# Three parts of a split product share one block of turned weights

## The chip, the cores and the metric

One core of a Trainium2 chip runs the whole program. The metric is the device time of one execution in microseconds (us). The parts named here are TensorE (matmuls), VectorE, ScalarE, GpSimd, and SyncE, whose queue issues all DMAs of this kernel, the DMA transposes among them.

## The reference

A decoder block over 16 batches of 100 tokens with 128 features. It has three parts, each followed by a residual sum and a layer norm: a self-attention of one head, a cross-attention, and a feed-forward part with product keys (8 heads, the 8 best of 1024 experts). The change is in the cross-attention:

```
q = layernorm(x) @ Wq                       # 16 heads of 64, per batch 100 tokens
k, v = split(layernorm(ctx) @ Wkv)          # ctx: 1444 rows of 128 features a batch
q = q * (1 + scale) + shift
attn = softmax(q @ k^T / 8)                 # 16 heads x 100 queries x 1444 keys
out = (attn @ v) @ Wout
```

The inputs are float32. The kernel works with the normed context itself in place of k and v (Wk is folded into the queries, Wv and Wout into one matrix), and holds each float32 number x as two float16 numbers, high = f16(x) and low = f16(x - high). A product of two such numbers is taken as three: high x high, high x low and low x high.

## The kernel before

`front` does the self-attention and prepares the first batch's context, `cross` does the cross-attention, `ffn` the rest. `cross` goes through 208 query tiles, 13 a batch: a batch has 16 x 100 = 1600 queries, so 12 tiles have 128 and the last has 64. Tile t is number i = t % 13 of its batch b. The order of work on each engine is written out by hand as one loop over t, with semaphores between the engines:

- TensorE, `scores(t)`: nine matmuls of up to 512 columns into three of six banks of PSUM, the 1444 scores of 128 queries.
- VectorE, `maximum(t)` (L887): the row maximum, and a small bias from it (L889).
- ScalarE, `exponent(t)` (L823): e32 = exp(score + bias), float32, two buffers. `high_half(t)` (L831): its float16 copy into p[., 0, .], three buffers.
- GpSimd for i in 0, 3, 4, 7 (L785), VectorE for the nine others (L896), a step later: `low_half(t)`, e32 minus the high half, into p[., 1, .].
- SyncE, `turn_high(t)` and `turn_low(t)` (L736, L742): two DMA transposes, which put 12 blocks of 128 keys by 128 queries each into pT, a ring of six tiles. 1444 keys are 11 blocks and a rest of 36; the rest of block 12 is zero.
- TensorE, `values(t)` (L999, L1000, L1003), four steps later: 12 blocks x 3 matmuls, which sum the context weighted with the turned weights into a quarter of one bank. L1003 of the first block waits for the low turn.
- ScalarE, `take_values` (L840): after each group of four tiles it copies that bank to uT; the next group's first matmul waits for this. The groups start at tiles 0, 4, 8 and 12 of a batch.

Between these go query jobs for the next batch (TensorE, then four copies on ScalarE, L850, L859, then GpSimd, L777), output jobs for the batch before (TensorE L965, VectorE L906, L910), and the next contexts: `context_load` (L519, L521, behind the turns of tile 0), statistics on VectorE (L534, L542, L547), `context_rstd` and `context_norm` on GpSimd, `context_hi` on ScalarE behind tile 4, `context_lo` on GpSimd at tile 5, and `turn_context` (L728) behind the turns of tiles 5 and 6. SyncE has one queue in this fixed order: an issue that waits holds all behind it.

The context's rows lie so that partition p has rows 11p to 11p + 10 in blocks 0 to 10. The last 36 rows lie in block 11 on partitions 0 to 35. `rows_of(n)` gives the partitions of block n in use: 128, or 36.

Of the kernel before, what the change touches and what calls it, by code (L numbers as in the profile page):

```python
# [6 lines left out]
F16 = mybir.dt.float16  # L7
# [16 lines left out]
HQ = H * S  # L24
PW = NTILE * P
NM = (HQ + P - 1) // P
LN3 = 1.0986122886681098
# [460 lines left out]
class Context:  # L488
# [3 lines left out]
    def __init__(self, sb, sem):  # L492
        self.raw = [sb(f"raw{i}", [P, NTILE, D]) for i in range(2)]
        self.cst = sb("cst", [P, NTILE, 6])
        self.cmv = [sb(f"cmv{i}", [P, NTILE, 2]) for i in range(2)]
        self.cve = sb("cve", [P, NTILE])
        self.crs = [sb(f"crs{i}", [P, NTILE]) for i in range(2)]
        self.xh = sb("xh", [P, NTILE, D])
        self.xa_hi = [sb(f"xa_hi{i}", [P, NTILE, D], F16) for i in range(2)]
        self.xa_lo = [sb(f"xa_lo{i}", [P, NTILE, D], F16) for i in range(2)]  # L500
        self.ctx_ld = [sem(f"ctx_ld{i}") for i in range(2)]
        self.init_done, self.ctx_stat, self.ctx_rstd, self.xh_done = (sem(n) for n in ("init_done", "ctx_stat", "ctx_rstd", "xh_done"))
        self.xa_hi_done, self.xa_lo_done = sem("xa_hi_done"), sem("xa_lo_done")
        self.pv_done = sem("pv_done")

        self.dve_waited = sem("dve_waited")


def context_init(pool, c):

    pool.memset(c.xh[:, :, :], 1.0).then_inc(c.init_done, 1)
    for i in range(2):
        pool.memset(c.cmv[i][:, :, :], 1.0).then_inc(c.init_done, 1)


def context_load(sp, c, a, bt):

    src = a["ctx_1024"][bass.ds(bt.index(), 1), :, :].rearrange("a t d -> (a t) d")
    sp.dma_start(c.raw[bt.par][:, 0:TF, :],  # L519
                 src[0:TF * P, :].rearrange("(p j) d -> p j d", j=TF)).then_inc(c.ctx_ld[bt.par], 16)  # L520
    sp.dma_start(c.raw[bt.par][0:TR, TF, :], src[TF * P:T, :]).then_inc(c.ctx_ld[bt.par], 16)  # L521


def context_stats(dve, c, bt, part):

    if part == 0:
        dve.wait_ge(c.ctx_ld[bt.par], bt.val(16, 32 - 16 * bt.par))
        if bt.off >= 2:
            dve.wait_ge(c.xh_done, bt.val(1, -1))
            dve.wait_ge(c.ctx_rstd, bt.val(1, 0))  # L530
# [26 lines left out]
def context_norm(dve, c, bt, part):  # L557
    if part == 0:
        dve.wait_ge(c.ctx_rstd, bt.val(1, 1))
        if bt.off >= 1:  # L560
            dve.wait_ge(c.xa_lo_done, bt.val(1, 0))
    for n in range(4 * part, 4 * part + 4):
        r = rows_of(n)
# [11 lines left out]


def context_lo(pool, c, bt):
    pool.wait_ge(c.xa_hi_done, bt.val(1, 1))
# [6 lines left out]
def rows_of(n):  # L585
    return P if n < TF else TR

# [75 lines left out]
def cross(nc, a, m, ps):  # L663
# [6 lines left out]
    with ExitStack() as ctx:  # L670
# [3 lines left out]
        def sem(name):  # L674
# [12 lines left out]
        e32 = [sb(f"e32_{i}", [P, T]) for i in range(E_BUF)]  # L687
        p = [sb(f"p{i}", [P, 2, PW], F16) for i in range(P_BUF)]
        pT = sb("pT", [P, RING, 2 * NTILE, P], F16)
        uT = sb("uT", [D, HQ])  # L690
# [3 lines left out]

        cx = m["context"]
        xa_hi, xa_lo, xh_done, xa_hi_done, xa_lo_done, pv_done, dve_waited = (
            cx.xa_hi, cx.xa_lo, cx.xh_done, cx.xa_hi_done, cx.xa_lo_done, cx.pv_done, cx.dve_waited)
# [3 lines left out]
        s_rdy, max_done, bias_done = sem("s_rdy"), sem("max_done"), sem("bias_done")  # L701
        e_done, hi_done, lo_dve, lo_pool = sem("e_done"), sem("hi_done"), sem("lo_dve"), sem("lo_pool")
        xT_ld = sem("xT_ld")
# [18 lines left out]
        def _(sp):  # L722
# [8 lines left out]
            def turn_high(t):  # L731
                rows = tile_rows(t % NM)
                sp.wait_ge(hi_done, t + 1)
                if t >= RING:
                    sp.wait_ge(pv_done, t - RING + 1)
                sp.dma_start_transpose(pT[:, t % RING, 0:NTILE, 0:rows.stop - rows.start],  # L736
                                       p[t % P_BUF][rows, 0, :]).then_inc(pT_hi_ld[t % RING], 16)

            def turn_low(t):
                rows = tile_rows(t % NM)  # L740
                sp.wait_ge(lo_pool if t % NM in POOL_LO else lo_dve, lo_of(t))
                sp.dma_start_transpose(pT[:, t % RING, NTILE:2 * NTILE, 0:rows.stop - rows.start],  # L742
                                       p[t % P_BUF][rows, 1, :]).then_inc(pT_lo_ld[t % RING], 16)

# [18 lines left out]
        def _(pool):  # L763
# [16 lines left out]
            def low_half(t):  # L780
                rows = tile_rows(t % NM)
                pool.wait_ge(hi_done, t + 1)
                if t >= P_BUF:
                    pool.wait_ge(pT_lo_ld[(t - P_BUF) % RING], 16 * ((t - P_BUF) // RING + 1))
                pool.tensor_tensor(out=p[t % P_BUF][rows, 1, 0:T], in0=e32[t % E_BUF][rows, :], in1=p[t % P_BUF][rows, 0, 0:T],  # L785
                                   op=ALU.subtract).then_inc(lo_pool, 1)

# [5 lines left out]
            for k in range(P_BUF):  # L793
                pool.memset(p[k][:, :, T:PW], 0.0).then_inc(pad_done, 1)
            queries_lo(0, 0)
# [21 lines left out]
        def _(act):  # L817
            def exponent(t):
                rows = tile_rows(t % NM)
                act.wait_ge(bias_done, t + 1)  # L820
                if t >= E_BUF:
                    act.wait_ge(lo_pool if (t - E_BUF) % NM in POOL_LO else lo_dve, lo_of(t - E_BUF))
                act.activation(e32[t % E_BUF][rows, :], score_banks(t)[rows, 0:T], ACT.Exp,  # L823
                               bias=bias[rows, t % N_BUF:t % N_BUF + 1]).then_inc(e_done, 1)

            def high_half(t):
# [3 lines left out]
                act.wait_ge(e_done, t + 1)  # L830
                act.activation(p[t % P_BUF][rows, 0, 0:T], e32[t % E_BUF][rows, :], ACT.Copy).then_inc(hi_done, 1)  # L831

# [48 lines left out]
        def _(dve):  # L881
# [9 lines left out]
            def low_half(t):  # L891
                rows = tile_rows(t % NM)
                dve.wait_ge(hi_done, t + 1)
                if t >= P_BUF:
                    dve.wait_ge(pT_lo_ld[(t - P_BUF) % RING], 16 * ((t - P_BUF) // RING + 1))
                dve.tensor_tensor(out=p[t % P_BUF][rows, 1, 0:T], in0=e32[t % E_BUF][rows, :], in1=p[t % P_BUF][rows, 0, 0:T],  # L896
                                  op=ALU.subtract).then_inc(lo_dve, 1)

# [26 lines left out]
            def layer_norm(b):  # L925
                dve.wait_ge(y_rstd, b + 1)
                dve.tensor_scalar(x2[:, b, :], acc[:, :], ymv[:, 0:1], yrs[:, 0:1], ALU.subtract, ALU.mult).then_inc(y_norm, 1)

            for part in range(4):
                context_stats(dve, cx, Batch(None, 1), part)  # L930
            for part in range(3):
                context_norm(dve, cx, Batch(None, 1), part)
            for t in range(ALL_TILES + DRAIN):
# [8 lines left out]
                if i in STAT_SLOTS and b + 2 < B:  # L942
                    context_stats(dve, cx, Batch(None, b + 2), STAT_SLOTS.index(i))
                if i == 6 and b or t == ALL_TILES + DRAIN - 1:
                    layer_norm(b - 1)

        @block.tensor
        def _(pe):
# [39 lines left out]
            def values(t):  # L988
# [6 lines left out]
                w = tile_cols(i).stop - tile_cols(i).start  # L995
                for n in range(NTILE):
                    hi, lo = xa_hi[b % 2][:, n, :], xa_lo[b % 2][:, n, :]
                    ph, pl = pT[:, t % RING, n, 0:w], pT[:, t % RING, NTILE + n, 0:w]
                    pe.matmul(out, hi, ph, start=n == 0, stop=False)  # L999
                    pe.matmul(out, lo, ph, start=False, stop=False)  # L1000
                    if n == 0:
                        pe.wait_ge(pT_lo_ld[t % RING], 16 * (t // RING + 1))
                    last = pe.matmul(out, hi, pl, start=False, stop=n == NTILE - 1)  # L1003
                last.then_inc(pv_done, 1)
# [618 lines left out]
```

## Time and profile before

| | us |
|---|---|
| median of 3 runs | 1376.27 (1375.0 to 1378.77) |
| the profiled execution | 1373.3 |
| its span | 1371.5 |
| TensorE matmuls busy | 1176.9 (86%) |
| VectorE busy | 1116.3 (81%) |
| ScalarE busy | 849.1 (62%) |
| GpSimd busy | 618.9 (45%) |
| SyncE's turns of the weights | 416 issues |

The profile is of one execution. Busy time is the union of an engine's instructions. A matmul's duration there is that of its way through the engine (about 0.22 us), and several are under way at once, so the distance between two starts tells what one costs. SyncE only issues, so it has no busy time; its issues are in the timeline with their durations. The idle time before an instruction stands behind it in brackets with what ended it.

### The profile page before, as it was taken

What the parts mean: (1) busy time and instruction counts of PE and PEld (TensorE: products, weight loads), DVE (VectorE), ACT (ScalarE), POOL (GpSimd) and SP (SyncE); (2) the same over time, 40 slices, a digit from 0 to 9 for tenths busy, and PEclk for the clock granted to TensorE, in tenths of its full rate; (3) what the DMA queues carried; (4) which work ended last, traced back from release to release, by engine and by line L of the source; (5) the groups of instructions that cost most, each with busy time, mean ns of one, the idle gap of its engine ahead of it and who ended that gap; (6) DMA issues with size and microseconds to landing.
All of it is one profiled execution on the core that took longest, in us unless ns stands there. A gap on an engine that the chain in (4) does not pass through costs nothing. (4 is left out here: it accounts for less than half of the span.)

```text
span 1371.5 us, 32769 instructions
## 1 busy us (share of the span) xinstructions
PE 1176.9 (86%) x13174; PEld 923.8 (67%) x13174; DVE 1116.3 (81%) x2700; ACT 849.1 (62%) x994; POOL 618.9 (45%) x445
## 2 busy tenths in 40 slices
PE   3567999998999999999999999999997547777788
PEld 2454677776777767777776777677775526776678
DVE  5886888887889888897888888888885278999984
ACT  0347778877778786777778778887773531222121
POOL 2254856566475666656476575667230000000000
PEclk9768999999999999999999999999998665666656
DMA  7016999999999999999999999999997200000000
GB/s 150 1 38 131 193 199 198 190 196 194 195 188 197 195 191 197 196 189 192 201 195 194 194 193 196 191 190 190 188 190 139 69 1 1 5 5 5 5 5 6
DMA packets 695185, 191.77 MB, mean 140 GB/s; under 512 B 681045, under 2 KB 692601, under 8 KB 694905
## 3 DMA queue, kind: packets, MB, share of 16 engines
q1 hardware_dynamic: 695032, 189.67, 81.5%
q8 instruction: 104, 1.70, 0.5%
q14 instruction: 49, 0.39, 0.1%
HBM read 18.92 MB, written 0.82 MB: 14 GB/s over the span
## 5 line engine op out<-in xcount | busy, mean ns | idle before, releaser
L1003 PE MATMUL ps<-pT,xa_hi 128*128 128x128 f16 (+1 forms) x2496 | 415.9, 217 | 27.2 <-DMA pT<-p 26.9
L999 PE MATMUL ps<-pT,xa_hi 128*128 128x128 f16 (+1 forms) x2496 | 417.5, 217 | 21.4 <-ACT uT L840 20.1
L823 ACT ACTIVATE e<-ps,bias 128x1444 f32<-128x1444 f32 (+1 forms) x208 | 305.4, 1468 | 194.4 <-DVE bias L889 194.1
L887 DVE TENSOR_REDUCE nmax<-ps 128x1 f32<-128x1444 f32 (+1 forms) x208 | 344.5, 1656 | 95.3 <-PE ps L985 94.2
L1000 PE MATMUL ps<-pT,xa_lo 128*128 128x128 f16 (+1 forms) x2496 | 417.6, 217 | 0.0
L831 ACT ACTIVATE p<-e 128x1444 f16<-128x1444 f32 (+1 forms) x208 | 294.5, 1416 | 8.5 <-DMA pT<-p 0.5
L896 DVE TENSOR_TENSOR p<-e,p 128x1444 f16<-128x1444 f32 x144 | 268.1, 1862 | 11.4 <-ACT p L831 7.8
L999 PEld LDWEIGHTS ps<-pT,xa_hi 128*128 128x128 f16 x2496 | 242.8, 98 | 49.4 <-issue 33.6
L785 POOL TENSOR_TENSOR p<-e,p 128x1444 f16<-128x1444 f32 x64 | 187.5, 2930 | 180.3 <-ACT p L831 178.4
L1003 PEld LDWEIGHTS ps<-pT,xa_hi 128*128 128x128 f16 x2496 | 242.7, 98 | 34.1 <-DMA pT<-p 33.8
L1000 PEld LDWEIGHTS ps<-pT,xa_lo 128*128 128x128 f16 x2496 | 242.7, 98 | 13.1
L983 PE MATMUL ps<-xT_hi,q_hi 128*128 128x512 f16 (+1 forms) x624 | 229.7, 368 | 8.0 <-DMA xT_lo<-xa_lo 7.2
L984 PE MATMUL ps<-xT_hi,q_lo 128*128 128x512 f16 (+1 forms) x624 | 229.6, 368 | 0.0
L985 PE MATMUL ps<-xT_lo,q_hi 128*128 128x512 f16 (+1 forms) x624 | 229.3, 368 | 0.0
L777 POOL TENSOR_TENSOR q_lo<-q,q_hi 128x400 f16<-128x400 f32 x64 | 102.7, 1605 | 181.5 <-ACT q_hi L859 181.5
L564 POOL TENSOR_SCALAR xh<-raw,cmv,crs 128x127 f32<-128x127 f32 x168 | 169.0, 1019 | 0.0
L1516 PE MATMUL ps<-mv_hi,oneh 128*128 128x16 f16 (+1 forms) x832 | 109.7, 215 | 44.9 <-DVE mv_lo L1437 44.9
L1516 PEld LDWEIGHTS ps<-mv_hi,oneh 128*128 128x128 f16 (+1 forms) x832 | 109.1, 175 | 47.8 <-DVE mv_lo L1437 47.3
L1153 POOL TENSOR_TENSOR comb<-top 128x512 f32<-128x512 f32 (+1 forms) x13 | 13.7, 1070 | 220.9 <-DVE top L1339 220.9
L1517 PEld LDWEIGHTS ps<-mv_lo,oneh 128*128 128x128 f16 (+1 forms) x832 | 109.0, 175 | 1.1 <-issue 1.0
L1517 PE MATMUL ps<-mv_lo,oneh 128*128 128x16 f16 (+1 forms) x832 | 109.4, 214 | 0.0
L985 PEld LDWEIGHTS ps<-xT_lo,q_hi 128*128 128x128 f16 x624 | 61.3, 98 | 66.4 <-issue 1.3
(219 smaller groups left out, 1794.9 us busy)
## 6 DMA issues: line engine op xcount, KB each, us to landing
raw<-in_ctx SPq DMA_DIRECT2D x16, 704.0 KB
pT<-p SPq DMA_TRANSPOSE x416, 4.5
f_wq<-in_L_ffn_w_q SPq DMA_DIRECT2D x1, 1024.0 KB, 4.9
f_wqt<-in_ffn_wq_t SPq DMA_DIRECT2D x2, 512.0 KB, 7.0
x_tok<-in_x SPq DMA_DIRECT2D x1, 800.0 KB
out_x<-ost SPq DMA_DIRECT2D x6, 128.0 KB, 1.8
wk_t<-in_wk_t SPq DMA_DIRECT2D x1, 512.0 KB, 5.9
wq_t<-in_wq_t SPq DMA_DIRECT2D x1, 512.0 KB, 8.2
```

The lines of the kernel that those rows point to most:

```text
L823: act.activation(e32[t % E_BUF][rows, :], score_banks(t)[rows, 0:T], ACT.Exp, bias=bias[rows, t % N_BUF:t % N_BUF + 1]).then_inc(e_done, 1)
L831: act.activation(p[t % P_BUF][rows, 0, 0:T], e32[t % E_BUF][rows, :], ACT.Copy).then_inc(hi_done, 1)
L887: dve.tensor_reduce(nmax[rows, k:k + 1], score_banks(t)[rows, 0:T], AX_X, ALU.max, negate=True).then_inc(max_done, 1)
L896: dve.tensor_tensor(out=p[t % P_BUF][rows, 1, 0:T], in0=e32[t % E_BUF][rows, :], in1=p[t % P_BUF][rows, 0, 0:T], op=ALU.subtract).then_inc ...
L983: pe.matmul(out, hi, xT_hi[b % 2][:, keys], start=True, stop=False)
L984: pe.matmul(out, lo, xT_hi[b % 2][:, keys], start=False, stop=False)
L985: last = pe.matmul(out, hi, xT_lo[b % 2][:, keys], start=False, stop=True)
L999: pe.matmul(out, hi, ph, start=n == 0, stop=False)
L1000: pe.matmul(out, lo, ph, start=False, stop=False)
L1003: last = pe.matmul(out, hi, pl, start=False, stop=n == NTILE - 1)
L1516: pe.matmul(dst, oneh[0:j, :, s], mv_hi[0:j, 0:nb, s], start=True, stop=False)
L1517: last = pe.matmul(dst, oneh[0:j, :, s], mv_lo[0:j, 0:nb, s], start=False, stop=True)
```

## The change

The products of the last 36 keys are high x high, high x low and low x high as well, and need three matmuls of a block that is three quarters zero. After the change one block holds all three: the weights' rest as high, high, low in three stretches of 36 columns, and the context's rest as high, low, high on the partitions 0 to 35, 36 to 71 and 72 to 107. One matmul sums them. p becomes one row of 23 blocks: 11 high, the shared block, 11 low. `turn_high` turns 11 blocks, `turn_low` the other 12.

For this the context's last 36 rows are loaded three times, onto three stretches of partitions, and the statistics and the norm run on 108 partitions. VectorE makes `xa_mix` once a batch: the normed rest, less its high half where the column `lo_rows` is -1 (partitions 36 to 71). ScalarE copies the weights' 36 columns in a second instruction, twice side by side. The low half is done in two instructions.

```diff
+COPIES = 3
+PB = 2 * TF + 1
...
 def context_load(sp, c, a, bt):
...
-    sp.dma_start(c.raw[bt.par][0:TR, TF, :], src[TF * P:T, :]).then_inc(c.ctx_ld[bt.par], 16)
+    for k in range(COPIES):
+        sp.dma_start(c.raw[bt.par][k * TR:(k + 1) * TR, TF, :], src[TF * P:T, :]).then_inc(c.ctx_ld[bt.par], 16)
...
+def context_mix(dve, c, bt):
+    dve.wait_ge(c.xa_hi_done, bt.val(1, 1))
+    if bt.off >= 2:
+        dve.wait_ge(c.pv_done, NM * (bt.off - 1))
+    dve.scalar_tensor_tensor(out=c.xa_mix[bt.par][:, :], in0=c.xa_hi[bt.par][:, TF, :], scalar=c.lo_rows[:, 0:1],
+                             in1=c.xh[:, TF, :], op0=ALU.mult, op1=ALU.add).then_inc(c.xa_mix_done, 1)
...
 def rows_of(n):
-    return P if n < TF else TR
+    return P if n < TF else COPIES * TR
...
-        p = [sb(f"p{i}", [P, 2, PW], F16) for i in range(P_BUF)]
-        pT = sb("pT", [P, RING, 2 * NTILE, P], F16)
+        p = [sb(f"p{i}", [P, PB * P], F16) for i in range(P_BUF)]
+        pT = sb("pT", [P, RING, PB, P], F16)
...
             def turn_high(t):
...
-                sp.dma_start_transpose(pT[:, t % RING, 0:NTILE, 0:rows.stop - rows.start],
-                                       p[t % P_BUF][rows, 0, :]).then_inc(pT_hi_ld[t % RING], 16)
+                sp.dma_start_transpose(pT[:, t % RING, 0:TF, 0:rows.stop - rows.start],
+                                       p[t % P_BUF][rows, 0:TF * P]).then_inc(pT_hi_ld[t % RING], 16)
             def turn_low(t):
...
-                sp.dma_start_transpose(pT[:, t % RING, NTILE:2 * NTILE, 0:rows.stop - rows.start],
-                                       p[t % P_BUF][rows, 1, :]).then_inc(pT_lo_ld[t % RING], 16)
+                sp.wait_ge(again_hi, t + 1)
+                sp.dma_start_transpose(pT[:, t % RING, TF:PB, 0:rows.stop - rows.start],
+                                       p[t % P_BUF][rows, TF * P:PB * P]).then_inc(pT_lo_ld[t % RING], 16)
...
             def high_half(t):
...
-                act.activation(p[t % P_BUF][rows, 0, 0:T], e32[t % E_BUF][rows, :], ACT.Copy).then_inc(hi_done, 1)
+                act.activation(p[t % P_BUF][rows, 0:TF * P], e32[t % E_BUF][rows, 0:TF * P], ACT.Copy).then_inc(hi_done, 1)
+                if t >= P_BUF:
+                    act.wait_ge(pT_lo_ld[(t - P_BUF) % RING], 16 * ((t - P_BUF) // RING + 1))
+                n = rows.stop - rows.start
+                act.activation(p[t % P_BUF][rows, TF * P:TF * P + 2 * TR].rearrange("q (c k) -> q c k", c=2),
+                               e32[t % E_BUF][rows, TF * P:T].rearrange("q (c k) -> q c k", c=1).to_broadcast([n, 2, TR]),
+                               ACT.Copy).then_inc(again_hi, 1)
...
             def low_half(t):
...
-                dve.tensor_tensor(out=p[t % P_BUF][rows, 1, 0:T], in0=e32[t % E_BUF][rows, :], in1=p[t % P_BUF][rows, 0, 0:T],
-                                  op=ALU.subtract).then_inc(lo_dve, 1)
+                for out, keys in (((TF + 1) * P, slice(0, TF * P)), (TF * P + 2 * TR, slice(TF * P, T))):
+                    if out < (TF + 1) * P:
+                        dve.wait_ge(again_hi, t + 1)
+                    ins = dve.tensor_tensor(out=p[t % P_BUF][rows, out:out + keys.stop - keys.start], in0=e32[t % E_BUF][rows, keys],
+                                         in1=p[t % P_BUF][rows, keys], op=ALU.subtract)
+                ins.then_inc(lo_dve, 1)
...
+                if i == 6 and b + 1 < B:
+                    context_mix(dve, cx, Batch(None, b + 1))
...
             def values(t):
...
-                for n in range(NTILE):
+                if i == 0:
+                    pe.wait_ge(cx.xa_mix_done, b + 1)
+                for n in range(TF):
...
-                    last = pe.matmul(out, hi, pl, start=False, stop=n == NTILE - 1)
+                    pe.matmul(out, hi, pl, start=False, stop=False)
+                last = pe.matmul(out, xa_mix[b % 2][:, :], pT[:, t % RING, TF, 0:w], start=False, stop=True)
```

GpSimd's `low_half` is split in the same way. The column `lo_rows` is made once in `context_init` by three small GpSimd instructions.

## Rows read from the trace of the kernel before

**Rows 1.** The page's granted TensorE clock, in tenths, over 40 slices of the span.

```profile
PEclk9768999999999999999999999999998665666656
```

**Rows 2.** Busy time of one window: PE, PEld, DVE, ACT, POOL, clock, DMA share, GB/s.

```profile
104.80:1050.80 946.00, 893.16 (x10616) 676.47 (x10617) 794.03 (x1319) 734.81 (x810) 557.61 (x369) 1.00 1.14 191
```

**Rows 3.** Waits from 122 to 1050.8 us: engine and line, total us, times, longest.

```profile
ACT e L823 <- DVE bias L889: 183.3, 147, 3.0
POOL p L785 <- ACT p L831: 166.9, 59, 9.4
...
PE ps L1003 <- DMA pT<-p: 26.9, 31, 1.7
PE ps L999 <- ACT uT L840: 20.1, 35, 1.0
...
POOL p L785 <- DMA pT<-p: 1.8, 1, 1.8
DVE p L896 <- DMA pT<-p: 1.4, 2, 0.9
```

**Rows 4.** Waits of the SyncE queue in the same window.

```profile
SPq L736 <- ACT p L831: 66.3, 62, 2.8
```

**Rows 5.** Timeline of SyncE at a context load: start us, duration us, line.

```profile
531.73 0.87 SPq L519 DMA_DIRECT2D raw<-in_ctx  x1
532.64 0.40 SPq L521 DMA_DIRECT2D raw<-in_ctx  x1
533.14 2.54 SPq L736 DMA_TRANSPOSE pT<-p  x1
```

**Rows 6.** SyncE's lines over the span: duration ns min/median/max, first and last start.

```profile
L736 SPq DMA_TRANSPOSE pT<-p x208: 1246/1762/3280, 114.7 to 1043.1; - x104
L742 SPq DMA_TRANSPOSE pT<-p x208: 1302/1808/4261, 117.6 to 1044.7; - x104
L521 SPq DMA_DIRECT2D raw<-in_ctx x16: 384/398/407, 4.2 to 826.7; - x16
```

**Rows 7.** Timeline of SyncE at the two turns of a batch's last tile.

```profile
580.26 3.25 SPq L742 DMA_TRANSPOSE pT<-p  x1
583.60 1.25 SPq L736 DMA_TRANSPOSE pT<-p  x1
584.91 1.43 SPq L742 DMA_TRANSPOSE pT<-p  x1
```

**Rows 8.** Timeline of TensorE at three waits, idle time in brackets.

```profile
555.01 0.22 PE L999 MATMUL ps<-pT,xa_hi 128*128 128x128 f16 x1 [0.78 <-ACT uT L840]
...
555.18 0.22 PE L999 MATMUL ps<-pT,xa_hi 128*128 128x128 f16 x1
...
533.64 0.19 PE L999 MATMUL ps<-pT,xa_hi 128*128 128x64 f16 x1 [0.48 <-ACT uT L840]
...
533.73 0.19 PE L999 MATMUL ps<-pT,xa_hi 128*128 128x64 f16 x1
...
569.99 0.23 PE L1003 MATMUL ps<-pT,xa_hi 128*128 128x128 f16 x1 [1.43 <-DMA pT<-p]
```

**Rows 9.** Timeline of ScalarE ahead of the wait at 533.64.

```profile
531.53 1.48 ACT L823 ACTIVATE e<-ps,bias 128x1444 f32<-128x1444 f32 x1
...
536.45 0.22 ACT L840 ACTIVATE uT<-ps 128x64 f32<-128x64 f32 x1
536.64 1.41 ACT L831 ACTIVATE p<-e 128x1444 f16<-128x1444 f32 x1
```

**Rows 10.** Timeline of VectorE ahead of the wait at 555.01.

```profile
544.24 0.17 DVE L906 RECIPROCAL ry<-ps 100x1 f32<-100x1 f32 x1 [0.22 <-PE ps L965]
...
545.55 0.85 DVE L534 BATCH_NORM_STATS2 cst<-raw 128x6 f32<-128x128 f32 x4
546.33 1.64 DVE L887 TENSOR_REDUCE nmax<-ps 128x1 f32<-128x1444 f32 x1
...
548.08 2.79 DVE L896 TENSOR_TENSOR p<-e,p 128x1444 f16<-128x1444 f32 x1
```

## What the change does to the time: the prediction

> **What bounds the kernel now.** First the granted clock over the span [rows 1], then the window of the stage at full clock [rows 2]. The reader is to see that the middle 946 us of 1371.5, the cross-attention stage, are one steady state: TensorE at the full 2.4 GHz, busy for 893.2 us (94%), and the DMA share above 1 all the while. VectorE is busy for 794.0 us (84%), ScalarE for 734.8 us (78%). The change touches this stage and, by two small loads, the one before it.
>
> Next the waits of the stage [rows 3]. TensorE idles in two places only: 26.9 us before L1003, the first matmul that needs the low half of a tile's turned weights (they have not landed), and 20.1 us before L999, when the bank of values has not been emptied by ScalarE (uT). ScalarE (183.3 us of waiting for VectorE's bias) and GpSimd (166.9 us before its low halves) have room on average.
>
> The last engine to look at is SyncE's queue, which turns the weights. The view of waits gives it idle time [rows 4], but the timeline does not show it: each issue begins 0.04 to 0.1 us after the one before has ended [rows 5]. The sum agrees with the timeline. A batch has 13 turns of 1.762 us and 13 of 1.808 us [rows 6], two of the context of about the same length (3.6 us), loads of 0.87 and 0.40 us [rows 5], and some 30 gaps of 0.09 us: 46.4 + 3.6 + 1.3 + 2.7 = 54.0 us. A batch takes 946/16 = 59.1 us. The 5 us between are issues that last 3 us in place of 1.8, as the one at 580.26 [rows 7]. So I read two chains of nearly equal length: SyncE's turns, without slack, and TensorE's matmuls, which wait 3 us a batch (26.9 + 20.1 over 16). The waits for L1003 are the places where the first chain holds the second.
>
> **The change, part by part.** The sum is made against the profiled execution: 1373.3 us, span 1371.5. The median of the runs shown is 1376.3, 3.0 more; I add that at the end.
>
> *Two matmuls fewer a tile.* The 128-column value matmuls start 0.056 us apart (555.01 to 555.18 is three of them), the 64-column ones of a batch's last tile 0.03 us (533.64 to 533.73) [rows 8]. 192 tiles x 2 x 0.056 + 16 x 2 x 0.03 = 22.5 us of TensorE's time, 1.4 us a batch. All of it lies on TensorE's own chain. What takes some of it back are the waits that do not get shorter with it.
>
> *The uT waits grow.* They fall on the 5th and the 13th tile of a batch, where a group of four value tiles begins: 0.78 us at 555.01 and 0.48 us at 533.64 [rows 8]. At the 13th the bank is free when ScalarE's exponent at 531.53, which starts with no idle time before it, and the uT copy behind it are done [rows 9]. Ahead of that exponent now stands the second small copy of the high halves. ScalarE's nearest row is the 64-column uT copy at 536.45, 0.19 us before the next instruction; the long copy loses 36 of 1444 columns, 0.03 us. So ScalarE arrives 0.16 us later, TensorE 2 x 0.11 us earlier: the wait grows by 0.4 us. At the 5th tile the chain runs over VectorE, from TensorE's job at 544.24 over the statistics, the maximum, the low half at 548.08 (2.79 us) and the next maximum [rows 10] to the exponent and uT. It gets the split low half and the new mix. Four statistics of 128 columns take 0.78 us (545.55 to 546.33), 0.195 us each, 0.06 us above their columns; so the split costs 0.06 us and the mix, of 128 columns, about 0.2 us. Two value tiles of TensorE lie beside it (0.22 us), so this wait grows by 0.5 us. Together 0.9 us a batch, 14 us in all. Between these points VectorE's and ScalarE's additions (9 splits a batch, 0.16 us a tile) lie in their idle time.
>
> *The price from the Trainium skill.* Its page "VectorE: DVE Perf Modes" (section "The TRN2 errata — SBUF-src ops pay a fixed extra latency per instruction") gives ScalarE 224 cycles and VectorE about 151 cycles on top of the elements. For 72 and 36 elements that is 0.25 and 0.19 us, estimates from the page; by them the two waits would grow by 1.1 us a batch in place of 0.9, 3 us in all. No row of before shows either instruction.
>
> *SyncE's queue.* The high turn goes from 12 blocks to 11. If the issue follows the blocks, it is shorter by 1.762/12 = 0.147 us. The last tile of a batch has half the rows, and its two issues at 583.60 and 584.91 last 1.25 and 1.43 us [rows 7], 0.45 us less for half of the data, which is 0.075 us for a twelfth. And 1.25 us may be a floor, so that nothing is gained. I take 0.1 us, between the first two: 13 x 0.1 = 1.3 us a batch, 21 us in all (0 to 31). Against it stand two more loads of 18 KB a batch, 0.398 us of issue each and the gap, 0.9 us. They are issued right behind the 704 KB load, and the next turn (533.14) takes 2.54 us, 0.8 us more than the median, since it waits for that load [rows 5, 6]. The new issues fall into this time, so I price them at 0.1 us a batch; without that cover they cost 14 x 0.9 = 12.6 us. In the front stage two of them stand ahead of the attention's weights: 0 to 0.9 us, I take 0.5.
>
> *The same in the words of the skill.* "DMA: Bandwidth & Descriptors" (section "Rules for kernel authors") says to coalesce small transfers, since under 64 KB one pays mostly overhead. That speaks against three loads of 18 KB. The trace puts 0.398 us of SyncE's time on one; where it falls decides the price, and the page does not say.
>
> *The waits for the low half shrink.* SyncE's chain gets 1.2 us a batch faster. TensorE's gets 1.4 - 0.9 = 0.5 us faster. The difference, 0.7 us a batch, can come out of the 26.9 us (1.7 us a batch) of waits: 11 us at most. Since the waits come in lumps (1.43 us at 569.99), where a long issue falls, I take 9.
>
> *Edits at nothing.* ScalarE now waits for the low turn of three tiles before, as VectorE did before it wrote the same buffer. Behind it stand the next exponent and the query copies. Before the low halves the same wait cost 1.8 us on GpSimd and 1.4 us on VectorE [rows 3], and the low turn gets no later. If it bound at each group of query jobs, it would cost 0.3 us a batch. GpSimd's split hides in its 166.9 us [rows 3], and the low turn waits in SyncE's queue anyway. Statistics and norm on 108 rows in place of 36 have the same columns. Waits for the mix are satisfied tiles earlier, as it is made at tile 6 of the batch before. The FFN and what follows the stage are untouched.
>
> *Sum.* -22.5 + 14 - 9 + 0.5 = -17.0 us, 1.1 us a batch. Both chains allow it: SyncE's alone gives -19. 1373.3 - 17 = 1356; with the 3 us to the median, 1359.
>
> **Rivals.** *(A) TensorE alone sets the time.* The uT waits do not grow, as the exponent has slack, and the low-half waits shrink. For: 94% busy, and only 20.1 us of uT waits. Against: those waits end on an exponent with nothing idle before it. Then -22.5 - 9 + 0.5 = -31: 1345. Chance 0.17.
>
> *(B) Slower: SyncE's queue sets the time and the issue of a turn does not follow its blocks.* The place is the turn after the context load. The shorter high turn saves nothing (floor of 1.25 us), the two extra issues delay each turn behind them, and the queue has no idle time in which to catch up. 12.6 us in the stage and 0.9 us in front: +13.5, 1390. It decides from the point where the high turns save less than 0.9 us a batch, 0.07 us each, and the raw load no longer covers the issues. For: back-to-back issues, the 1.25 us floor. Against: a half tile's turns are shorter, and the 0.8 us beside the raw load. With half of the cover it is 1383. Chance 0.21.
>
> *(C) No change: what TensorE saves goes into waits.* The high turns save nothing and the loads are covered, so SyncE's chain stays at its length, and TensorE waits 1.4 us more a batch, at L1003 in place of L999. 1376, within 4 us. The same comes out if small instructions cost twice my price (uT waits +1.8 us a batch, -22.5 + 29 - 9 = -2). Chance 0.14.
>
> **How the numbers follow.** Forecast 0.48, A 0.17, C 0.14, B 0.21. The predicted time is the forecast's, 1359; its own range, from the SyncE term of 0.075 to 0.147 us and uT waits of 0.6 to 1.2 us a batch, is 1351 to 1367. The range for all is 1346 to 1383: it takes in most of A, all of C and the near part of B. 0.3% is 4 us, about what a measurement of this kernel tells from no change. Faster by more than that: the forecast and A, 0.65. Within: C, 0.14. Slower: B, 0.21.
>
> **What would show it.** Value matmuls 7072 in place of 7488, at the same distance. The median of L736's issue falls to about 1.66 us (0 saved: B or C; 1.61: the blocks count in full). The uT waits rise from 20 to some 34 us, the low-half waits fall from 27 to some 18. The copy of 72 columns takes about 0.2 us on ScalarE, VectorE's busy time in the stage rises by about 12 us. The turn behind the load stays near 2.5 us or falls towards 1.8, while the batch does not get longer. I am wrong if low-half waits grow (then SyncE's queue was the one bound, and its turns did not get shorter), or if uT waits stay where they are.

## The result, and the profile after

The changed kernel takes 1363.65 us (median of 4 runs, 1362.32 to 1367.09); the kernel before took 1376.36 beside it. The ratio is 0.991 (0.9885 to 0.9934): 12.7 us less. The forecast was 1359. The profiled execution of the changed kernel was the slowest of its four, 1367.1 us with a span of 1365.3, against 1373.3 and 1371.5. So the two traces differ by 6.2 us, half of what the medians do, and they are read for the places of the time, the medians for its size.

The first fence is the window of the stage after: busy time of PE, PEld, DVE, ACT, POOL, then clock, DMA share and GB/s, as in [rows 2]. The second has the waits from 122 to 1050.8 us, as in [rows 3].

```profile
104.80:1050.80 946.00, 873.56 (x10212) 660.55 (x10212) 836.80 (x1494) 757.63 (x1018) 559.62 (x433) 0.99 1.10 184
```

```profile
POOL p L811 <- ACT p L859: 172.2, 49, 9.9
ACT e L851 <- DVE bias L923: 160.6, 128, 3.5
...
PE ps L1042 <- ACT uT L874: 60.4, 48, 4.5
...
PE ps L1006 <- DVE acc L948: 2.9, 2, 1.4
...
PE ps L1046 <- DMA pT<-p: 0.9, 2, 0.7
```

L1042 is the old L999, L1046 the old L1003. TensorE is busy for 19.6 us less. Its waits for the low half, 26.9 us before [rows 3], are gone (0.9). Its waits for uT went from 20.1 us to 60.4. The three terms of the stage sum to -22.5 (the matmuls, as in the prediction) + 40.3 - 26.0 = -8.2 us. From the first score matmul to the last value matmul the stage took 945.9 us (104.8 to 1050.8) and now takes 938.7 (105.9 to 1044.6), 7.2 less, which agrees within 1 us; the front is 1.1 longer.

Of the 60.4 us of waits, 33.3 lie before the 5th tile of a batch, 15.2 before the 13th and 12.0 before the 9th, where it was 9.6, 9.7 and 0.8. VectorE is busy for 42.8 us more (794.0 in [rows 2]). Next, the split groups by shape, from 104.8 to 1050.8 us: count, busy us, mean ns, idle time before.

```profile
L933 DVE TENSOR_TENSOR p<-e,p 128x1408 f16<-128x1408 f32 x128 | 233.4, 1823 | 10.9 <-ACT p L859 8.5 <-issue 0.3
...
L863 ACT ACTIVATE p<-e 128x72 f16<-128x72 f32 x192 | 52.2, 272 | 0.0
L933 DVE TENSOR_TENSOR p<-e,p 128x36 f16<-128x36 f32 x128 | 48.9, 382 | 0.0
...
L811 POOL TENSOR_TENSOR p<-e,p 128x36 f16<-128x36 f32 x64 | 16.2, 253 | 0.0
L594 DVE SCALAR_TENSOR_TENSOR xa_mix<-xa_hi,lo_rows,xh 128x128 f16<-128x128 f16 x15 | 8.0, 533 | 0.0
```

VectorE's 36 columns take 0.38 us in the mean, and the mix 0.53, where I had priced 0.06 and 0.2. The mean hides two kinds: 95 of the 128 short instructions last 0.18 to 0.20 us and 33 last 0.93 or 0.94. One of the 33 lies in the first row here: the pair of low-half instructions, 1.62 us for 1408 columns and 0.94 for 36. The other rows are GpSimd's low half of the queries (q_lo), beside the pair and alone.

```profile
530.45 2.48 DVE L933 TENSOR_TENSOR p<-e,p 128x1408 f16<-128x1408 f32 x2 [0.32 <-ACT p L859]
531.07 1.80 POOL L800 TENSOR_TENSOR q_lo<-q,q_hi 128x400 f16<-128x400 f32 x1 [3.14 <-ACT q_hi L893]
551.94 0.94 POOL L800 TENSOR_TENSOR q_lo<-q,q_hi 128x400 f16<-128x400 f32 x1 [2.87 <-ACT q_hi L893]
```

q_lo starts while VectorE's long instruction runs (to 532.07), and lasts until 532.87, 0.80 us after it, in place of 0.94 us in all. The short instruction starts at 531.99, when q_lo is already under way, and ends at 532.92, 0.05 us after q_lo. So the engine that starts second gets its work done only when the other has ended, in both directions. Before the change the low half was one instruction: q_lo waited for it and nothing of the same low half stood behind q_lo. The split lets q_lo in between the two parts. 33 times 0.75 us are 25 us of VectorE's 42.8.

The mix and the low half beside GpSimd's low half of the context (xa_lo) show the same; start and duration in us.

```profile
137.37 2.48 DVE L933 TENSOR_TENSOR p<-e,p 128x1408 f16<-128x1408 f32 x2 [2.51 <-ACT p L859]
139.78 3.24 DVE L594 SCALAR_TENSOR_TENSOR xa_mix<-xa_hi,lo_rows,xh 128x128 f16<-128x128 f16 x1
...
545.38 1.65 DVE L921 TENSOR_REDUCE nmax<-ps 128x1 f32<-128x1444 f32 x1
547.06 0.15 DVE L923 TENSOR_SCALAR bias<-nmax 128x1 f32<-128x1 f32 x1
547.14 3.52 DVE L933 TENSOR_TENSOR p<-e,p 128x1408 f16<-128x1408 f32 x2
550.58 0.34 DVE L594 SCALAR_TENSOR_TENSOR xa_mix<-xa_hi,lo_rows,xh 128x128 f16<-128x128 f16 x1
```

```profile
137.99 1.81 POOL L800 TENSOR_TENSOR q_lo<-q,q_hi 128x400 f16<-128x400 f32 x1 [2.94 <-ACT q_hi L893]
139.76 3.11 POOL L602 TENSOR_TENSOR xa_lo<-xh,xa_hi 128x1536 f16<-128x1536 f32 x1
...
545.43 0.56 POOL L817 TENSOR_TENSOR yrs<-yve,nhalf 100x1 f32<-100x1 f32 x1
545.97 3.10 POOL L602 TENSOR_TENSOR xa_lo<-xh,xa_hi 128x1536 f16<-128x1536 f32 x1
```

The mix at 139.78 starts just after GpSimd's xa_lo (139.76), and ends (143.02) just after it (142.87); it took 3.24 us, and 0.34 at 550.58, with nothing beside it, as in all 14 batches behind the first. The pair of low-half instructions at 547.14 lasts 3.52 us; xa_lo ends at 549.07, and from there to the pair's end are 1.6 us, about what a pair takes (1.7). The reduction at 545.38 and the bias at 547.06 also lie beside xa_lo and are no longer than elsewhere. Nor does every instruction of GpSimd do it: 28 low halves that started beside its norm of the context (L576, one input tile) kept their 1.63 us, and VectorE's sums of the heads (L948, one input in PSUM) kept their 0.35 us beside GpSimd's low half. What the trace shows is this: xa_lo (all 14 low halves that started beside it, 3.06 to 3.66 us) and q_lo (33 of 33 short ones), each with two input tiles in SBUF, held the instructions of VectorE with two such inputs until they had ended. The low half of [rows 10], 2.79 us at 548.08, was already such a case (1.66 us alone): I read its length as its own. The end of the chain to the 5th tile is then set by xa_lo, which does not come earlier when TensorE does.

The waits have one more effect. The first fence is TensorE's timeline at a 5th tile, the second two windows of 34 value matmuls each: behind this wait, and behind a wait of another batch.

```profile
612.74 0.27 PE L1042 MATMUL ps<-pT,xa_hi 128*128 128x128 f16 x1 [2.00 <-ACT uT L874]
...
616.20 0.22 PE L1047 MATMUL ps<-pT,xa_mix 128*128 128x128 f16 x1
```

```profile
612.70:616.30 3.60, 3.56 (x35) 3.59 (x36) 2.27 (x9) 2.53 (x3) 2.37 (x1) 0.53 1.13 212
555.00:557.00 2.00, 1.94 (x35) 1.97 (x36) 1.97 (x9) 1.34 (x2) 0.74 (x1) 1.00 1.13 207
```

After 2.0 us without work the granted clock was 0.53 of full here, near the 1.2 GHz level, and the tile took 3.5 us in place of 1.9. Three later batches have this at the 5th tile; they last 59.3 us, the steady ones 57.7. The first batch has it too, from within its wait of 4.5 us on. In the trace of the kernel before it came once, behind waits of 0.83 and 1.67 us for turns.

Last, SyncE's two turns over the span (ns: minimum, median, maximum) and its queue's waits in the stage; before: [rows 6] and [rows 4].

```profile
L758 SPq DMA_TRANSPOSE pT<-p x208: 1236/1720/3260, 115.7 to 1038.2; - x104
...
L765 SPq DMA_TRANSPOSE pT<-p x208: 1217/1643/3013, 118.8 to 1039.5; - x104
```

```profile
SPq L758 <- ACT p L859: 84.6, 62, 2.6
SPq L765 <- DVE p L933: 37.9, 40, 2.9
SPq L765 <- POOL p L811: 27.6, 21, 1.8
```

The high turn, which lost a block, fell from 1.762 us to 1.720; the low turn, with its 12 blocks, from 1.808 to 1.643. Together that is 13 x 0.207 = 2.7 us a batch. And the queue, issue behind issue before (the issues filled 890 of the 932 us between the first turn and the last), has room: the gaps over 0.15 us between issues sum to 66 us in the stage, where they summed to 8.8.

### The profile page after: what moved, and what is told of

Same layout as the page of the kernel before. It is cut to its first block and busy times, and to the rows that moved or that the text cites. A ratio compares the mean times of both kernels' runs of the same rounds, so it can differ in the third digit from the quotient of the medians.

```text
span 1365.3 us, 32623 instructions
## 1 busy us (share of the span) xinstructions
PE 1152.9 (84%) x12753; PEld 905.5 (66%) x12758; DVE 1154.6 (85%) x2860; ACT 871.6 (64%) x1202; POOL 621.0 (45%) x512
## 5 line engine op out<-in xcount | busy, mean ns | idle before, releaser
L1042 PE MATMUL ps<-pT,xa_hi 128*128 128x128 f16 x2288 | 386.4, 219 | 60.4 <-ACT uT L874 60.4
L1046 PE MATMUL ps<-pT,xa_hi 128*128 128x128 f16 x2288 | 386.6, 219 | 0.9 <-DMA pT<-p 0.9
L1043 PE MATMUL ps<-pT,xa_lo 128*128 128x128 f16 x2288 | 386.6, 219 | 0.0
L933 DVE TENSOR_TENSOR p<-e,p 128x1408 f16<-128x1408 f32 (+3 forms) x288 | 299.5, 1081 | 11.4 <-ACT p L859 8.5
L859 ACT ACTIVATE p<-e 128x1408 f16<-128x1408 f32 (+1 forms) x208 | 289.6, 1392 | 7.6
L1042 PEld LDWEIGHTS ps<-pT,xa_hi 128*128 128x128 f16 x2288 | 224.0, 99 | 91.7 <-issue 78.8
L811 POOL TENSOR_TENSOR p<-e,p 128x1408 f16<-128x1408 f32 (+1 forms) x128 | 196.6, 1557 | 183.7 <-ACT p L859 183.7
L1043 PEld LDWEIGHTS ps<-pT,xa_lo 128*128 128x128 f16 x2288 | 224.0, 99 | 12.2
L1046 PEld LDWEIGHTS ps<-pT,xa_hi 128*128 128x128 f16 x2288 | 224.1, 99 | 1.3 <-DMA pT<-p 1.3
L576 POOL TENSOR_SCALAR xh<-raw,cmv,crs 128x127 f32<-128x127 f32 x168 | 185.8, 1115 | 0.0
L800 POOL TENSOR_TENSOR q_lo<-q,q_hi 128x400 f16<-128x400 f32 x64 | 90.1, 1407 | 175.8 <-ACT q_hi L893 175.8
```

Source lines behind the costliest of these rows:

```text
L859: act.activation(p[t % P_BUF][rows, 0:TF * P], e32[t % E_BUF][rows, 0:TF * P], ACT.Copy).then_inc(hi_done, 1)
L933: ins = dve.tensor_tensor(out=p[t % P_BUF][rows, out:out + keys.stop - keys.start], in0=e32[t % E_BUF][rows, keys], in1=p[t % P_BUF][rows, ...
L1046: pe.matmul(out, hi, pl, start=False, stop=False)
```

## The experiments

Theory Q: SyncE's queue of turns held the kernel before, and the shorter turn makes the gain. Theory D: what the change gives back, it gives back through the added instructions on VectorE, by the uT waits. The rivals stand in the expectations; theory W there is D in its first form, and each of T, A, N and L is explained where it stands. The kernels ran beside the kernel before, in three rounds (its medians there: 1373.7, 1374.2, 1373.3), and each ratio is against that. The changed kernel was not in these rounds: where a run is compared with it, the size is given by the ratios and by the medians, and the two differ by 2 to 3 us. "Before" or "after" says which kernel is edited.

**Only the matmuls (before).** The values' high part times the rest's two matmuls are left out.

```
-                    pe.matmul(out, hi, ph, start=n == 0, stop=False)
-                    pe.matmul(out, lo, ph, start=False, stop=False)
+                    if n < TF:
+                        pe.matmul(out, hi, ph, start=n == 0, stop=False)
+                        pe.matmul(out, lo, ph, start=False, stop=False)
```

> The kernel before with 34 value matmuls a tile: the two matmuls of the rest block that take the high half of the weights are left out; turns, loads and all other instructions are those of before. Theory Q (SyncE's turns are a chain as long as TensorE's, and the low-half waits absorb what TensorE saves): low-half waits rise from 27 to 35 us or more, the time falls by 4 to 14 us only, 1362 to 1372. Rival T (TensorE alone sets the time): the full 22 us, 1354, with low-half waits at 27 us.

Measured: 1367.8, ratio 0.996 (0.9946 to 0.9973), 5.9 us less. The waits:

```profile
PE ps L1004 <- DMA pT<-p: 34.5, 48, 1.6
PE ps L1000 <- ACT uT L840: 26.4, 35, 1.6
```

TensorE lost 22.5 us of matmuls, and its two waits grew by 7.6 and 6.3 us: most of the work removed turned into waits, more of it into those for the turns, which is Q.

**Only the shorter turn (before).** The high turn has 11 blocks, and the rest's high matmuls read block 10.

```
-                sp.dma_start_transpose(pT[:, t % RING, 0:NTILE, ...
-                                       p[t % P_BUF][rows, 0, :])
+                sp.dma_start_transpose(pT[:, t % RING, 0:TF, ...
+                                       p[t % P_BUF][rows, 0, 0:TF * P])
```

> The kernel before with high turns of 11 blocks in place of 12; still 36 value matmuls, those of the rest block read block 10 again, so the high half of the last 36 keys is left out. Theory Q: the low-half waits fall from 27 us to under 10 and the time by about as much, 1356 to 1366, though TensorE does the same work. Rival T: no change, 1374 to 1378. If the issue of a turn does not follow its blocks, no change either, and the median of the high turn's issue stays at 1.76 us.

Measured: 1348.4, ratio 0.9812 (0.9789 to 0.9836), 25.3 us less, more than Q expected. The waits, and the two turns:

```profile
PE ps L999 <- ACT uT L840: 25.8, 47, 1.7
...
PE ps L1003 <- DMA pT<-p: 2.2, 4, 1.0
```

```profile
L736 SPq DMA_TRANSPOSE pT<-p x208: 1231/1722/2961, 115.8 to 1018.4; - x104
```

```profile
L742 SPq DMA_TRANSPOSE pT<-p x208: 1287/1716/3308, 118.7 to 1020.1; - x104
```

Both turns' medians are shorter, together by 0.132 us a tile: 13 x 16 x 0.132 = 27 us. That this is near the 25.3 measured is partly luck, since medians leave out the long issues: summed over all 416 turns the issues took 821.6 us before and 780.3 here, 41 less, and 15 of that came back as gaps over 0.15 us (8.8 before, 24.2 here), which leaves 26. One block less of 24 in the queue shows in every issue, not in its own. TensorE's own work is unchanged here, so it was the stream of turns that held the kernel. Whether the issues or the transfers behind them set its pace no run separates: a turn lands 4.5 us after its issue starts, so more than one is under way, and the DMA share is above 1 in both kernels.

**Both (before).**

> The kernel before with 34 value matmuls and high turns of 11 blocks, and none of the added instructions (no second copy, no split low half, no mix, no further loads); the high half of the last 36 keys is left out. Theory W (the added instructions lengthen the waits for uT, 20 to 60 us in the changed kernel, and these took back more than half of the gain): uT waits of 25 to 35 us here, low-half waits under 5, 1336 to 1346, so some 20 us under the changed kernel. Rival (the uT waits rise because TensorE comes earlier, the added instructions are hidden): uT waits of about 50 us or more and 1358 to 1364 as the changed kernel.

Measured: 1340.4, ratio 0.9762 (0.974 to 0.9783), 33.4 us less. This is the change without what it adds. It is 20.7 us more than the change brings (12.7): the price of the additions.

```profile
PE ps L1000 <- ACT uT L840: 34.4, 43, 1.8
```

So of the 40.3 us by which the uT waits grew in the changed kernel, 14.3 come without any addition, because TensorE and the queue are faster, and 26.0 with the additions.

**The shared block with a turn of 12 (after).** A block of zeros between the high blocks and the shared one makes the high turn 12 blocks long again; the matmuls stay at 34.

```
-PB = 2 * TF + 1
+PB = 2 * TF + 2
+SB = TF + 1
...
+                sp.dma_start_transpose(pT[:, t % RING, 0:SB, ...
+                                       p[t % P_BUF][rows, 0:SB * P])
```

> The changed kernel with high turns of 12 blocks again: a block of zeros stands between the 11 high blocks and the shared one, is turned with the high ones and read by no matmul. Theory Q (the shorter turn is what relieved TensorE): low-half waits of 10 us or more again in place of 0.9, the issues' median back at 1.76 to 1.80 us, 1368 to 1378, so little or nothing of the gain is left though TensorE still does 34 matmuls a tile. Rival T (the matmuls made the gain): within 0.3% of the changed kernel, 1360 to 1368.

Measured: 1373.6, ratio 0.9999 (0.9983 to 1.0016). The whole gain is gone. The low-half waits are back, the uT waits remain high:

```profile
PE ps L1044 <- ACT uT L876: 44.0, 38, 4.5
PE ps L1048 <- DMA pT<-p: 23.9, 37, 1.5
```

The issues' medians are back at 1.766 and 1.759 us, and the gaps over 0.15 us sum to 16 us in place of 66. With "only the shorter turn" this shows Q from both sides. The low turn's 1.759 is still below the 1.808 of before with the same number of blocks, so not all of an issue's length follows the blocks.

**Without the small low half (after).** The 36-column low-half instruction is left out on VectorE and GpSimd; its block holds zeros.

```
-                for out, keys in (((TF + 1) * P, ...), (TF * P + 2 * TR, ...)):
+                for out, keys in (((TF + 1) * P, slice(0, TF * P)),):
```

> The changed kernel without the second instruction of the low half (36 columns) on VectorE and GpSimd; the low half of the last 36 keys' weights is left out. The kernel with both parts and none of the added instructions took 1340.4 us, the changed one 1363.7, so the added instructions cost some 23 us. Theory D (most of them is VectorE's: the 36-column instruction starts while GpSimd works and lasts 0.93 us in place of 0.19 at two tiles a batch, and 0.1 us at seven): a fall of 8 to 16 us, uT waits from 60 to 45 us. Rival A (it is ScalarE's second copy): a fall of under 4 us.

Measured: 1344.7, ratio 0.978 (0.9759 to 0.9802), 29.5 us less than before and so 17 to 19 less than the changed kernel; VectorE's busy time in the stage is back at 802.0 us, the uT waits are 44.8. It is more than D expected, and nearly the whole price of the additions. The waits before the 5th tile fall from 33.3 to 19.7 us. How it divides between VectorE's and GpSimd's instruction was not tried.

**One copy on ScalarE (after).** The high part is one copy of 1444 columns; the second copy of the rest, and the wait before it, are left out.

```
+                act.activation(p[t % P_BUF][rows, 0:T], e32[t % E_BUF][rows, :], ACT.Copy)...
```

> The changed kernel with one copy of 1444 columns on ScalarE as before, and no second copy of the rest; the product of the high half of the rest with the context's low half is left out. Theory D: ScalarE's copy stands on the chain only ahead of the waits at the 9th and 13th tile, where the exponent starts with no idle time: a fall of 3 to 8 us. Rival A (0.16 us on ScalarE at each of 208 tiles is the main price): a fall of 12 to 20 us.

Measured: 1366.0, ratio 0.9937 (0.9915 to 0.9959): no gain on the changed kernel, where I had expected 3 to 8 us; the uT waits are 57.3. D as I had it, with the time lost to ScalarE's copy, falls. But the copy is not wholly in ScalarE's slack: the waits before the 9th and 13th tile fall by 5.3 us together (to 8.4 and 13.5), those before the 5th grow by 2.0 (to 35.3), and TensorE is at the lower clock behind the wait in four later batches in place of three. So the small gain at two places is lost again at the third. VectorE's (or GpSimd's) part of the additions remains as the price.

**The rest loaded once (after).** From the third batch on, the two more loads of 18 KB are left out.

```
-    for k in range(COPIES):
+    for k in range(COPIES if bt.off < 2 else 1):
```

> The changed kernel with the last 36 rows of the context loaded once a batch from the third batch on; the two other stretches keep rows of the first batches. Theory Q (the issues fall beside the 704 KB load, and SyncE's queue has idle time now): no change beyond 0.3%, 1360 to 1367. Rival L (each issue delays all turns behind it): a fall of 6 to 13 us.

Measured: 1365.2, ratio 0.9926 (0.9904 to 0.9947): no gain. Their issues are hidden:

```profile
529.42 0.91 SPq L529 DMA_DIRECT2D raw<-in_ctx  x1
530.69 1.12 SPq L532 DMA_DIRECT2D raw<-in_ctx  x3
531.91 1.36 SPq L758 DMA_TRANSPOSE pT<-p  x1
533.37 2.91 SPq L765 DMA_TRANSPOSE pT<-p  x1
```

The three take 1.12 us. The turn behind them has 1.36, and the long issue (2.91, as 2.54 before in [rows 5]) is one turn later.

**The mix two tiles later (after).** `i == 6` becomes `i == 8`.

> The changed kernel with the mix made at tile 8 of the batch before in place of tile 6, where VectorE soon has idle time; all else equal. Theory W: the uT wait before the 5th tile (2.01 us a batch) shrinks by the mix's 0.26 us and by more in the first batch, where the mix took 3.24 us; the stretches of TensorE at half clock behind that wait (1.6 us in three batches) may go: 1354 to 1361. Rival (the mix is not on the chain): 1363 to 1365, the wait stays at 2.0 us.

Measured: 1355.3, ratio 0.9874 (0.9852 to 0.9897), 5 us below the changed kernel by the ratios and 8 by the medians, with intervals that overlap; the uT waits are 55.4, and the 4.5 us wait of the first batch (behind the mix at 139.78) is 2.0. In the later batches the wait before the 5th tile falls from 2.0 to 1.75 us, and no tile behind it runs at the lower clock.

**VectorE's 36 columns first (after).** The small instruction waits for ScalarE's second copy and then runs before the long one, in place of behind it.

```
-  for out, keys in (((TF + 1) * P, slice(0, TF * P)), (TF * P + 2 * TR, slice(TF * P, T))):
+  for out, keys in ((TF * P + 2 * TR, slice(TF * P, T)), ((TF + 1) * P, slice(0, TF * P))):
```

> The changed kernel with one change of order: VectorE's 36-column instruction of the low half ahead of the 1408-column one; GpSimd's stays behind. Theory D (what costs is that the small one starts while GpSimd works): it lasts 0.19 us at tiles 1 and 9 in place of 0.93, the uT waits fall by some 8 us, 1350 to 1358. Rival N (the number of instructions costs, not their place): 1360 to 1366.

Measured: 1356.2, ratio 0.988 (0.9855 to 0.9904), 4 us below the changed kernel by the ratios, 7 by the medians, again with overlapping intervals. Here the group by shape:

```profile
L933 DVE TENSOR_TENSOR p<-e,p 128x1408 f16<-128x1408 f32 x128 | 208.5, 1629 | 0.0
L933 DVE TENSOR_TENSOR p<-e,p 128x36 f16<-128x36 f32 x128 | 49.0, 382 | 24.6 <-ACT p L863 22.2
```

The short one keeps its mean of 0.38 us; the long one falls from 1.82 us to 1.63. VectorE waits 22 us for the second copy and is still ahead. The equal mean of the short one is chance: only 2 now start behind q_lo in place of 33, but 15 start beside xa_lo and last 1.19 us (median), for which the long one behind them no longer pays. All in all less of VectorE's work starts into GpSimd's.

**xa_lo before the other jobs of GpSimd (after).** At the 5th tile GpSimd makes xa_lo before the small power yrs and the query jobs, and so it is over 0.56 us earlier.

```
+                if i == 5 and more:
+                    context_lo(pool, cx, Batch(None, b + 1))
                 for kind, of, g in jobs_of(t):
```

> The changed kernel with one change of order on GpSimd: at tile 5 the low half of the context ahead of the small power of the output norm, so that it begins and ends 0.56 us earlier. Theory D: VectorE's low half of that time is 2.8 us in place of 3.4 and the uT wait before the 5th tile 0.5 us shorter in each batch: 1352 to 1359. Rival: nothing, 1360 to 1366.

Measured: 1354.1, ratio 0.9854 (0.9828 to 0.988), 8 to 10 us below the changed kernel, with intervals that do not overlap; uT waits 53.3. VectorE's long low half still starts beside xa_lo, but lasts 2.88 us (median) in place of 3.41; the waits before the 5th tile fall from 33.3 to 26.1 us.

**The same (before).**

> The kernel before with the same change of order on GpSimd (the low half of the context ahead of the small power). Theory Q: before the change the low-half waits take up what the uT waits give, since SyncE's queue has no slack: within 0.3% of before, 1370 to 1378. Rival (the uT wait before the 5th tile is paid in full there too): 1362 to 1368.

Measured: 1372.2, ratio 0.999 (0.9975 to 1.0006): no change. The waits only move:

```profile
PE ps L1003 <- DMA pT<-p: 29.3, 35, 2.2
PE ps L999 <- ACT uT L840: 16.2, 33, 1.0
```

As long as the queue holds, a shorter chain over VectorE is worth nothing (uT 20.1 to 16.2, low half 26.9 to 29.3). Once the queue has room, the same edit brings 8 to 10 us. This pair shows that the bound has moved.

**All three orders together (after).** Mix at tile 8, small instruction first, xa_lo first. Nothing of the computation is left out.

> The changed kernel, complete, with three changes of order: the mix at tile 8, VectorE's 36-column instruction ahead of the long one, and at tile 5 GpSimd's low half of the context ahead of its small power. Theory D: the low half at tile 5 of VectorE waits for GpSimd 0.56 us less, the 36-column instruction lasts 0.19 us at all tiles; the uT wait before the 5th tile falls from 2.0 to about 1.1 us, in all 12 to 20 us less than the changed kernel: 1342 to 1352. Rival (the order within VectorE does not matter, only the number of instructions): as with the mix at tile 8 alone, 1355.

Measured: 1343.4 (1342.0 to 1344.9), ratio 0.977 (0.9748 to 0.9792). It beats both kernels, the kernel before by 30.8 us and the changed one by 18 to 20, and is within 4 us of the change without its additions. The waits before the 5th tile are 16.7 us in all, 16.4 in that kernel.

```profile
PE ps L1042 <- ACT uT L874: 43.0, 48, 2.0
```

```profile
L933 DVE TENSOR_TENSOR p<-e,p 128x1408 f16<-128x1408 f32 x128 | 216.6, 1692 | 0.0
L933 DVE TENSOR_TENSOR p<-e,p 128x36 f16<-128x36 f32 x128 | 40.5, 316 | 21.7 <-ACT p L863 19.1
```

## Why the prediction was right, and where not

**The result** lies 4.7 us above the forecast and within its own range (1351 to 1367). The mechanism is the one forecast: two chains, both shortened, and part of TensorE's saving lost to uT waits. Rival A fell, since the uT waits tripled. B fell, since SyncE's issues did get shorter. C as first put fell by the same; but its second condition, small instructions at twice my price, came true and more (uT waits +2.5 us a batch, where it had +1.8). Its result did not, because the low-half waits fell by 26 us and not by 9. So three terms were wrong in size, the two largest errors (+26 and -17 us) with opposite signs, and that the sum came within 5 us is in good part luck.

**The matmuls, -22.5.** The count holds (TensorE 19.6 us less busy), and I wrote that waits would take some of it back. Alone it is worth 5.9 us.

**SyncE's queue.** I took 0.1 us a high turn (-21 us), with the blocks in full as the far end (-31). The run with only the shorter turn says 25 us, from issues of both turns. The median of L736 (1.72 measured, 1.66 foretold) was therefore the wrong thing to look at: its 0.04 us a tile are 9 us, and two thirds of the gain would be missed. I also used the term only as a leave for TensorE's sum. It was the one that counted: -25 us alone, and without it nothing is left of the gain in the changed kernel.

**The low-half waits, -9.** Measured -26.0. The difference of the two chains a batch was taken with a uT term that was too small; TensorE came later than I thought, and the queue was faster.

**The uT waits, +14.** Measured +40.3, a new wait at the 9th tile included (0.8 to 12.0 us). The step that failed is the price of the split and the mix on VectorE: +12 us of busy time foretold, +42.8 measured. I had foretold that part of the waits would grow by TensorE's earlier arrival, and 14.3 us of it need no addition; the other 26.0 do. I priced split and mix by statistics, which no work of GpSimd's stretches, and the nearest row of the same kind, 2.79 us for one low half, stood in [rows 10]; that such an instruction takes 1.66 us alone I did not look up. And the split does not only add its own time: it lets GpSimd in between.

"VectorE: DVE Perf Modes" of the Trainium skill (section "The TRN2 errata — SBUF-src ops pay a fixed extra latency per instruction"), weighed in the prediction, gives VectorE about 151 cycles on top of the elements, an estimate of 0.19 us for 36. The trace agrees for the 95 short instructions that start free of q_lo (0.18 to 0.20 us); the mean of 0.38 comes from the 33 others, so the fixed cost was not what was missing. For ScalarE's 72 columns the estimate from the page's 224 cycles is 0.25 us, the trace has 0.272; but without this copy the time did not change.

**The loads, +0.1 a batch, and the front, +0.5.** Hidden, as foretold; the front took 1.1. "DMA: Bandwidth & Descriptors" of the Trainium skill (section "Rules for kernel authors") says to coalesce small transfers. Here two more of 18 KB a batch cost nothing that a run here could tell.

**Edits at nothing.** ScalarE's new wait for the low turn does not appear among the waits of the stage.

**Open.** Why one block less shows in the low turn's issue and hardly in its own, and whether the issues or the transfers set the pace of the turns; how the small instruction's price divides between the engines; and how much of the uT waits' price is the lower clock behind them, which no run isolated (in the trace of the changed kernel the three later batches that have it are 3 x 1.6 = 4.8 us longer in all).

## What to carry to other kernels

Where a queue issues without a gap in the timeline, its length is the first term, and what is taken from another engine is worth little until the queue is shorter. After such a relief the next chain counts, and edits that were worth nothing before are worth trying again. Price a small added instruction by where it starts, beside which work of its neighbour, and ask what a cut in a long instruction lets in. Try its order before its removal: here the additions cost 21 us, and three changes of order brought 18 of them back.

## What the hardware showed

Where VectorE's low half or mix and GpSimd's q_lo or xa_lo met, all with two input tiles in SBUF, the one that started second was not done before the other had ended. VectorE's mix beside xa_lo took 3.24 us in place of 0.34, its 36 columns beside q_lo 0.94 in place of 0.19, and GpSimd's q_lo beside VectorE's low half 1.80 in place of 0.94. A reduction and a one-input instruction of VectorE beside xa_lo did not stretch, and GpSimd's small power of one column (0.57 us) held nothing: without the small low half 14 mixes started beside it and took 0.34 us. And after waits of 2.0 us TensorE ran one tile at about 1.2 GHz in some batches, 1.6 us more each, and in others not.
